# W and its sums stored two pairs at a time: batch 0 of an adapted mixture-of-LoRA kernel

## The chip, the core and the metric

The kernel runs on one core of a Trainium2 chip. The metric is the device time of one execution in microseconds (us), the median of the runs. Five engines are spoken of: PE (TensorE), DVE (VectorE), ACT (ScalarE), POOL (GpSimd) and SP (SyncE), which here only issues DMAs. PE's clock is granted at one of two levels, 1.2 or 2.4 GHz; a granted clock of 1.00 is the higher.

## What is computed

```python
# x (8, 512, 2048), W (2048, 2048), all float32
x = x + einsum('bnr,bor->bno', einsum('bni,bri->bnr', x, B0[ids]), A0[ids])     # rank 16
base = einsum('btd,od->bto', x, W)
logits = einsum('btd,ed->bte', x, Wr) + 5 * one_hot(language_ids)
gates = scatter(softmax(top_2(logits)))                                        # 8 experts
h = einsum('btd,erd->bter', x, A)
out = x + base + 2 * einsum('bter,bte,eor->bto', h, gates, Bm)
```

## The kernel before

Each float32 operand is split into a high and a low part (float32r), and each product is three matmuls: high by high, low by high, high by low (`three_products`). Batches 1 to 7 multiply x and W (plus the identity, for the residual x) by a scheme with seven products over halves instead of eight. The seven combinations of blocks of W that it needs are made in batch 0 and stored in the internal tensor `t_scr`; each later batch reads them back as 56 pairs and 4 LoRA pairs (`pair_load`).

Batch 0 runs over 36 slots, four chunks of nine: in slot i, PE multiplies pair i by the whole of x (`first_products`, 24 matmuls of 512 columns), and slots 8, 17, 26 and 35 are LoRA slots (`first_gated`, 12 matmuls). Everything else is laid out around these slots by hand, in `pe_main`, `act_main`, `dve_main` and `sp_main`, and every engine runs its own list in order:

- SP loads raw W for slot i+5 in slot i (`first_load`, L602, four pieces; L598, two pieces of the LoRA rows from `bt_scr`) into one of two buffers, `raw[:, g % 2]`. It also loads x of batch 1 (`x_load`, L280, eight pieces in each of slots 4 to 7 and 10 to 21) and stores finished output (L763).
- PE transposes W for slot i+3 in slot i in two halves (`w_transpose`, L626): the first half at the head of the slot, the second in the middle.
- ACT copies the transposed blocks to one of two kept places (`w_keep`, L637); DVE makes four sums of the blocks (`w_sums`, L646 to L651) into `tst`; SP stores the direct blocks (`w_store`, L660 and L661) and the sums (`w_sums_store`, L666).
- ACT and DVE split pair i+2 in slot i into high and low parts (`pair_hi`, L715, and `pair_lo`, L719) in a ring of three places. `pair_hi(g)` waits until PE has used pair g-3.
- In slots 9 to 25 the x of batch 1 is turned (`x_turn`), split (`x_hi`, `x_lo`) and multiplied with the small weights (`aux_products`).
- DVE adds the identity to a loaded block of W where it lies on the diagonal (`add_identity`, L612).

The loads wait like this, where `c_wl` counts the low parts made and `c_wt` the halves transposed:

```python
            if g >= 2:
                if (g - 2) % 9 == 8:
                    e.wait_ge(c_wl, g - 1)
                else:
                    e.wait_ge(c_wt, 2 * w_number(g - 2) + 2)
```

`w_number(g)` numbers the pairs without the LoRA ones. `SLOTS0` is 36.

Of the kernel before, what the change touches and what calls it, by code (L numbers as in the profile page):

```python
# [5 lines left out]
def adapted_moe_lora_kernel(nc, x, adapter_ids, language_ids, A0, B0, W, Wr, A, Bm, out):  # L6
# [42 lines left out]
    t_scr = nc.dram_tensor("t_scr", (NI, 2, KP, P, 2, CW), f32, kind="Internal").ap()  # L49
# [16 lines left out]
    LAST = pair_of(NB, 0)  # L66

# [21 lines left out]
    with ctx:  # L89
# [60 lines left out]
        wh = sb("wh", [P, RING, 2, CW], f32r)  # L150
        wl = sb("wl", [P, RING, 2, CW], f32r)
# [14 lines left out]
        gxl, gx = late[:, 0:NAUX], late[:, 256:256 + NAUX]  # L166
        gs = [late[:, 512 + 256 * s:512 + 256 * s + NAUX] for s in range(2)]
# [135 lines left out]

        def x_hi(e, n, u):
# [324 lines left out]
        def w_keep(e, g, h):  # L629
            w = w_number(g)  # L630
            if h == 0 and w >= 2:
                before = g - 2 - (g % 9 < 2)
                e.wait_ge(c_wl, before + 1)
                e.wait_ge(c_t, 4 * w - 4)
                e.wait_ge(d_bs[w % 2], 32 * (w // 2))
            e.wait_ge(c_wt, 2 * w + h + 1)
            e.copy(w_kept(g)[:, h, :], pb[:, 6 + h, :]).then_inc(c_wc, 1)  # L637

        def w_sums(e, g):
            w = w_number(g)  # L640
            b11, b12 = w_kept(g)[:, 0, 0:HT], w_kept(g)[:, 0, HT:CW]
            b21, b22 = w_kept(g)[:, 1, 0:HT], w_kept(g)[:, 1, HT:CW]
            e.wait_ge(c_wc, 2 * w + 2)
            if w:
# [899 lines left out]
```

## Time and profile before

| | |
|---|---|
| median of 3 runs | 1641.58 us (1640.65 to 1642.41) |
| the profiled execution | 1641.15 us |
| its span | 1639.3 us |
| PE busy | 1587.2 us, 97% of the span |
| DVE busy | 1185.9 us, 72% |
| ACT busy | 751.0 us, 46% |
| DMA, mean over the span | 214 GB/s |
| mean granted clock of PE | 0.989 |

The profile is of one execution. Busy shares are means over stages with different limits: batch 0 ends near 355 us, and the seven later batches take about 183 us each. A row of the timeline gives start, duration, engine, line and operation, and in brackets the idle time of the engine just before it and what ended it.

### The profile page before, as it was taken

How to read it: one execution, taken by the hardware profiler on the slowest of the kernel's cores; microseconds unless marked ns; L12 is line 12 of the kernel's file. 1: busy time of each engine (PE TensorE's matmuls, PEld its weight loads, DVE VectorE, ACT ScalarE, POOL GpSimd, SP SyncE). 2: the span in 40 equal slices, each digit the busy share in tenths (PEclk: the TensorE clock that was granted, in tenths of full speed). 3: DMA queues.
4: the chain of work that ended last, by engine and by line, in shares of the span. 5: the costliest groups of instructions: out<-in, count | busy, mean ns of one | idle time of the engine just before them, and what ended most of it. 6: DMA issues, size and time to landing. Idle time of an engine off the chain costs nothing.

```text
span 1639.3 us, 21144 instructions
## 1 busy us (share of the span) xinstructions
PE 1587.2 (97%) x7680; PEld 1333.1 (81%) x7680; DVE 1185.9 (72%) x1615; ACT 751.0 (46%) x984; POOL 10.1 (1%) x19
## 2 busy tenths in 40 slices
PE   7798989999999999999999999999999999999998
PEld 5676768778888888888888888888888888888887
DVE  3674444578769877788769877788769877787665
ACT  4553233335544544445444544445444544445443
POOL 1100000000000000000000000000000000000000
PEclk9898999999999999999999999999999999999999
DMA  8689888968967787878878798878877798566664
GB/s 247 187 218 220 190 194 195 229 211 216 218 199 232 218 232 200 227 227 222 210 205 234 211 233 203 220 236 216 212 207 234 212 241 196 198 226 209 207 220 160
DMA packets 429626, 351.32 MB, mean 214 GB/s; under 512 B 285210, under 2 KB 358218, under 8 KB 428490
## 3 DMA queue, kind: packets, MB, share of 16 engines
q1 hardware_dynamic: 427346, 345.77, 77.7%
q10 hardware_dynamic: 2176, 4.19, 0.9%
q8 instruction: 61, 1.00, 0.3%
q14 instruction: 43, 0.35, 0.1%
HBM read 280.62 MB, written 68.82 MB: 213 GB/s over the span
## 4 chain that ended last, share of the span: by engine, by line
PE 85%; SPq 6%; DMA 4%; DVE 2%; ACT 1%; issue 1%; ACTq 0%; DVEq 0%
PE pb L724 25%; PE pb L723 25%; PE pb L725 25%; PE pb L337 4%; PE pb L339 3%; SPq L602 2%; SPq L280 2%; PE pb L491 2%; DMA raw<-in_L_cond_W_dram 1%; DMA t_scr<-tst 1%; PE pb L626 1%; DMA wrn<-in_L_cond_Wr_dram 1%; DMA t_scr<-raw 0%; SPq L666 0%; DMA bt_scr<-bt 0%
## 5 line engine op out<-in xcount | busy, mean ns | idle before, releaser
L715 ACT CAST wh<-raw 128x1024 fp32r<-128x1024 f32 (+1 forms) x456 | 477.1, 1046 | 684.2 <-PE pb L725 678.4
L719 DVE TENSOR_TENSOR wl<-raw,wh 128x1024 fp32r<-128x1024 f32 (+1 forms) x456 | 554.7, 1216 | 299.2 <-ACT wh L715 298.9
L723 PE MATMUL pb<-wh,sh 128*128 128x512 f32 x1568 | 612.8, 391 | 0.5 <-DVE ost L759 0.5
L724 PE MATMUL pb<-wl,sh 128*128 128x512 f32 x1568 | 611.5, 390 | 0.0
L725 PE MATMUL pb<-wh,sl 128*128 128x512 f32 x1568 | 611.1, 390 | 0.0
L725 PEld LDWEIGHTS pb<-wh,sl 128*128 128x128 f32 x1568 | 294.3, 188 | 62.7
L723 PEld LDWEIGHTS pb<-wh,sh 128*128 128x128 f32 x1568 | 294.5, 188 | 56.2 <-DVE wl L719 0.9
L724 PEld LDWEIGHTS pb<-wl,sh 128*128 128x128 f32 x1568 | 294.6, 188 | 55.0
L337 PE MATMUL pb<-awb,xah 128*128 128x304 f32 x512 | 138.5, 304 | 2.7 <-DVE aux L352 1.6
L339 PE MATMUL pb<-awb,xal 128*128 128x256 f32 x512 | 134.5, 280 | 0.0
L723 PE MATMUL pb<-wh,xh 128*128 128x512 f32 x256 | 109.0, 426 | 1.1 <-DVE xl L513 1.1
L724 PE MATMUL pb<-wl,xh 128*128 128x512 f32 x256 | 104.7, 409 | 0.0
L725 PE MATMUL pb<-wh,xl 128*128 128x512 f32 x256 | 104.2, 407 | 0.0
L337 PEld LDWEIGHTS pb<-awb,xah 128*128 128x128 f32 x512 | 96.3, 188 | 7.6 <-DVE aux L352 1.8
L339 PEld LDWEIGHTS pb<-awb,xal 128*128 128x128 f32 x512 | 96.3, 188 | 4.2
L565 DVE TENSOR_TENSOR sl<-pool_a,sh 128x512 fp32r<-128x512 f32 x120 | 82.1, 685 | 0.0
L637 ACT COPY raw<-pb 128x512 f32<-128x512 f32 x64 | 37.5, 588 | 93.4 <-PE pb L626 50.6
L560 ACT CAST sh<-pool_a 128x512 fp32r<-128x512 f32 x120 | 73.5, 613 | 0.0
L316 DVE TENSOR_TENSOR xal<-pool_a,xah 128x512 fp32r<-128x512 f32 x88 | 60.3, 686 | 15.9 <-ACT xah L311 15.6
L498 DVE TENSOR_TENSOR pool_a<-pool_a,pb 128x512 f32<-128x512 f32 x88 | 59.3, 681 | 11.7 <-PE pb L491 11.7
L626 PE MATMUL pb<-ident,raw 128*128 128x128 f32 x256 | 41.3, 286 | 26.8 <-DMA raw<-in_L_cond_W_dram 17.5
L311 ACT CAST xah<-pool_a 128x512 fp32r<-128x512 f32 x88 | 54.5, 621 | 26.0 <-DVE pool_a L264 16.0
(135 smaller groups left out, 1277.3 us busy)
## 6 DMA issues: line engine op xcount, KB each, us to landing
raw<-t_scr SPq DMA_DIRECT2D x392, 512.0 KB, 4.3
xst<-in_x_dram SPq DMA_DIRECT2D x896, 32.0 KB, 3.6
raw<-in_L_cond_W_dram SPq DMA_DIRECT2D x128, 128.0 KB, 4.2
t_scr<-tst SPq DMA_DIRECT2D x32, 512.0 KB, 5.4
raw<-bt_scr SPq DMA_DIRECT2D x28, 512.0 KB, 3.7
out_dram<-ost SPq DMA_DIRECT2D x28, 512.0 KB, 4.3
out_dram<-u SPq DMA_DIRECT2D x28, 512.0 KB, 3.4
t_scr<-raw SPq DMA_DIRECT2D x32, 256.0 KB, 2.9
```

What stands on the lines that cost most here:

```text
L316: e.tensor_tensor(out=xal[:, u % 2, :, :].rearrange("p k t -> p (k t)"), in0=two(n, q, kp), in1=xah[:, u % 2, :, :].rearrange("p k t -> p ...
L337: e.matmul(pb[:, 4 + t, 0:2 * AW], xah[:, u % 2, k, toks], cols[:, 0:2 * AW], start=u % 8 == 0 and k == 0, stop=False)
L339: last = e.matmul(pb[:, 4 + t, 0:LOW], xal[:, u % 2, k, toks], cols[:, 0:LOW], start=False, stop=u % 8 == 7 and k == 1)
L498: e.tensor_tensor(out=two(n, q, kp), in0=two(n, q, kp), in1=pb[:, delta_bank(n, u), :], op=ALU.add)\
L560: e.copy(sh[:, h % SR, :, :].rearrange("p k t -> p (k t)"), two(b, SUM_QUARTER[product], kp)).then_inc(c_sph, 1)
L565: e.tensor_tensor(out=sl[:, h % SR, :, :].rearrange("p k t -> p (k t)"), in0=two(b, SUM_QUARTER[product], kp), in1=sh[:, h % SR, :, :].rea ...
L626: last = e.transpose(pb[:, 6 + h, j * P:(j + 1) * P], w_raw(g)[:, j, h, :], ident[:, :])
L715: e.copy(pair_split(wh, g), pair_source(g)).then_inc(c_wh, 1)
L719: e.tensor_tensor(out=pair_split(wl, g), in0=pair_source(g), in1=pair_split(wh, g).bitcast(f32), op=ALU.subtract).then_inc(c_wl, 1)
L723: e.matmul(o, h, wh[:, g % RING, k, :], start=start, stop=False)
L724: e.matmul(o, h, wl[:, g % RING, k, :], start=False, stop=False)
L725: return e.matmul(o, l, wh[:, g % RING, k, :], start=False, stop=stop)
```

## The change

Two pairs of W (two slots) share a kept place and a store. A kept place, and the buffers of the sums, hold for each block the columns of both pairs side by side, so that a store writes runs of 2048 bytes where it wrote 1024; `t_scr` is laid out accordingly, and batches 1 to 7 read each half-pair as two runs of 256 words. There is a second kept pair of places (`kept1`), and it lies where one of the three places of the ring was: during batch 0 the ring of split parts has two places, `pair_hi` and `pair_lo` of pair i+1 stand in slot i, and from batch 1 on it has three again. The sums have two buffers of two sums each (`tst`, `tst1`); `tst1` lies over the second buffer of the split x, so batch 1's x is split in one buffer. `gs` and `gx` move into `bt`, and `late` into `ost`. In `sp_main` the load of pair 8 goes behind that of pair 9.

```diff
@@ ring @@
+    def ring(g):
+        return g % 2 if g < SLOTS0 else g % RING
+
+    def ring_before(g):
+        return g - 2 if g < SLOTS0 + 2 else g - RING
@@ places @@
-    t_scr = nc.dram_tensor("t_scr", (NI, 2, KP, P, 2, CW), f32, kind="Internal").ap()
+    t_scr = nc.dram_tensor("t_scr", (NI, 2, KP, P, 2, 2, HT), f32, kind="Internal").ap()
-        wh = sb("wh", [P, RING, 2, CW], f32r)
-        wl = sb("wl", [P, RING, 2, CW], f32r)
+        sb("places", [P, 2, 2, CW], f32, s5)
+        kept1 = sb("kept1", [P, 2, 2, CW], f32, s5)
+        whl = sb("whl", [P, 2 * RING, 2, CW], f32r)
+        def w_high(n):
+            return whl[:, n, :, :]
+        def w_low(n):
+            return whl[:, (4, 5, 3)[n], :, :]
-        gxl, gx = late[:, 0:NAUX], late[:, 256:256 + NAUX]
-        gs = [late[:, 512 + 256 * s:512 + 256 * s + NAUX] for s in range(2)]
+        gxl, gx = bt[:, HO:HO + NAUX], bt[:, HO + 256:HO + 256 + NAUX]
+        gs = [bt[:, HO + 512 + 256 * s:HO + 512 + 256 * s + NAUX] for s in range(2)]
@@ x_hi @@
-            if 16 * n + u >= 2:
+            if n == 1:
+                e.wait_ge(c_ax, 16 + u)
+            elif 16 * n + u >= 2:
                 e.wait_ge(c_ax, 16 * n + u - 1)
@@ w_keep @@
-            if h == 0 and w >= 2:
-                before = g - 2 - (g % 9 < 2)
+            if h == 0 and w >= 4 and w % 2 == 0:
+                before = g - 3 - (g % 9 < 3)
                 e.wait_ge(c_wl, before + 1)
-                e.wait_ge(c_t, 4 * w - 4)
-                e.wait_ge(d_bs[w % 2], 32 * (w // 2))
+                e.wait_ge(c_t, 4 * (w - 2))
+                e.wait_ge(d_bs[w // 2 % 2], 32 * (w // 4))
@@ w_sums @@
-            if w:
-                e.wait_ge(d_ts, 16 * w)
+            if w == 0:
+                e.wait_ge(c_ax, 16)
+            elif w % 2 == 0:
+                e.wait_ge(d_ts, 32 * (w // 2))
@@ w_store, w_sums_store @@
-            e.dma_start(w_place(g, 0, 2), w_kept(g)[:, :, 0:HT]).then_inc(d_bs[w % 2], 16)
-            e.dma_start(w_place(g, 6, 1), w_kept(g)[:, 1:2, HT:CW]).then_inc(d_bs[w % 2], 16)
+            kept = w_kept2(g).rearrange("p h o w n -> p h o (w n)")
+            e.dma_start(w_place(g, 0, 2), kept[:, :, 0, :]).then_inc(d_bs[w // 2 % 2], 16)
+            e.dma_start(w_place(g, 6, 1), kept[:, 1:2, 1, :]).then_inc(d_bs[w // 2 % 2], 16)
-            e.dma_start(w_place(g, 2, 4), tst[:, :, :]).then_inc(d_ts, 16)
+            for n in range(2):
+                e.dma_start(w_place(g, 2 + 2 * n, 2), w_sum2(n)).then_inc(d_ts, 16)
@@ pair_hi @@
-            if g >= RING:
-                wait_used(e, g - RING)
+            if g == SLOTS0 + 2:
+                e.wait_ge(c_wl, SLOTS0 - 1)
+                e.wait_ge(c_t, 4 * 32)
+                e.wait_ge(d_bs[1], 32 * 8)
+            elif g >= 2:
+                wait_used(e, ring_before(g))
@@ three_products @@
+        def part(place_of, g, k):
+            t = place_of(ring(g))
+            if g >= SLOTS0 and not is_lora(*place(g)):
+                return t.rearrange("p a (k n) -> p k a n", k=2)[:, k, :, :]
+            return t[:, k, :]
-            e.matmul(o, h, wh[:, g % RING, k, :], start=start, stop=False)
+            e.matmul(o, h, part(w_high, g, k), start=start, stop=False)
...
@@ bt_copy @@
             e.wait_ge(c_bt, q + 1)
+            if q == 0:
+                e.wait_ge(c_ax, 16)
+                e.wait_ge(d_gs, 32)
+                e.wait_ge(d_ag, 48)
@@ dve_start @@
             pair_lo(e, 0)
-            w_sums(e, 0)
...
             g_lo(e)
+            w_sums(e, 0)
             w_sums(e, 1)
@@ sp_start @@
             first_load(e, 2)
-            w_store(e, 0)
-            w_sums_store(e, 0)
             first_load(e, 3)
             w_store(e, 1)
...
-            w_store(e, 2)
@@ act_main; dve_main has the same with pair_lo @@
-                pair_hi(e, i + 2)
+                if i:
+                    pair_hi(e, i + 1)
@@ sp_main @@
-                if i + 2 < SLOTS0 and (i + 2) % 9 != 8:
+                if i + 2 < SLOTS0 and (i + 2) % 9 != 8 and w_number(i + 2) % 2:
                     w_sums_store(e, i + 2)
...
-                if i + 5 < SLOTS0:
+                if i == 4:
+                    first_load(e, 9)
+                    first_load(e, 8)
+                elif i + 5 < SLOTS0 and i != 3:
                     first_load(e, i + 5)
...
-                if i + 3 < SLOTS0 and (i + 3) % 9 != 8:
+                if i + 3 < SLOTS0 and (i + 3) % 9 != 8 and w_number(i + 3) % 2:
                     w_store(e, i + 3)
```

The instructions move on SP's queue at two places. In slots 3 to 5 the list of before reads as follows; L598 is the load of pair 8, which waits for `bt_scr` (`d_bt`), and the L602 behind it is W(9).

```order
L1042 DMA bt_scr<-bt 128x2048 [waits c_btc]
L1046 DMA bt_scr<-late 128x1024 [waits c_btc]
L598 DMA raw<-bt_scr 128x256 [waits d_bt,c_wt]
L598 DMA raw<-bt_scr 128x256
L660 DMA t_scr<-raw 128x2x256 [waits c_wc]
L661 DMA t_scr<-raw 128x256
L666 DMA t_scr<-tst 128x4x256 [waits c_t]
L602 DMA raw<-in_L_cond_W_dram 128x2x128 [waits c_wt]
L602 DMA raw<-in_L_cond_W_dram 128x2x128 x3
```

The same stretch of SP's list in the changed kernel (L648 is the load of W, L644 that of pair 8, L305 a piece of x, L709, L710 and L716 the stores), as far as W(10), the L648 that waits for `c_wl`:

```order
L1109 DMA bt_scr<-bt 128x2048 [waits c_btc]
L1113 DMA bt_scr<-ost 128x1024 [waits c_btc]
L648 DMA raw<-in_L_cond_W_dram 128x2x128 [waits c_wt]
L648 DMA raw<-in_L_cond_W_dram 128x2x128 x3
L644 DMA raw<-bt_scr 128x256 [waits d_bt,c_wt]
L644 DMA raw<-bt_scr 128x256
L305 DMA xst<-in_x_dram 32x8x32 [waits c_bt]
L305 DMA xst<-in_x_dram 32x8x32 x7
L709 DMA t_scr<-kept 128x2x512 [waits c_wc]
L710 DMA t_scr<-kept 128x512
L716 DMA t_scr<-tst 128x2x512 [waits c_t]
L648 DMA raw<-in_L_cond_W_dram 128x2x128 [waits c_wl]
```

W(9) now stands ahead of pair 8, and the stores are wider and come once in two slots.

DVE's list in slots 6 and 7 of before, where the `wl` of 128x512 is the low part of pair 8 and the `wl` behind it that of pair 9:

```order
L719 TENSOR_TENSOR wl<-raw,wh 128x512 [waits c_wh]
L498 TENSOR_TENSOR pool_a<-pool_a,pb 128x512 [waits c_dl]
L513 TENSOR_TENSOR xl<-pool_a,xh 128x2x256 [waits c_h0]
L438 TENSOR_TENSOR gate<-ohw 128x32 [waits c_gd]
L441 TENSOR_TENSOR auxl<-aux,gate 128x128 [waits c_gd]
L441 TENSOR_TENSOR auxl<-aux,gate 128x128 x3
L719 TENSOR_TENSOR wl<-raw,wh 128x1024 [waits c_wh]
L646 TENSOR_TENSOR tst<-raw 128x256 [waits d_ts,c_wc]
```

DVE's list at the same place in the changed kernel (L775 is `pair_lo`):

```order
L775 TENSOR_TENSOR whl<-kept,whl 128x1024 [waits c_wh]
L530 TENSOR_TENSOR pool_a<-pool_a,pb 128x512 [waits c_dl]
L545 TENSOR_TENSOR xl<-pool_a,xh 128x2x256 [waits c_h0]
L470 TENSOR_TENSOR gate<-ohw 128x32 [waits c_gd]
L473 TENSOR_TENSOR auxl<-aux,gate 128x128 [waits c_gd]
L473 TENSOR_TENSOR auxl<-aux,gate 128x128 x3
L775 TENSOR_TENSOR whl<-raw,whl 128x512 [waits c_wh]
L693 TENSOR_TENSOR tst<-raw 128x256 [waits d_ts,c_wc]
```

The low part of pair 8 (128x512) has moved from slot 6 to slot 7, behind the small operations.

## Rows read from the trace of the kernel before

**Rows 1.** Stretches: us; busy PE, PEld, DVE, ACT, POOL; clock, DMA share, GB/s

```profile
120.00:262.00 142.00, 121.46 (x595) 100.76 (x594) 66.56 (x131) 43.98 (x67) 0.00 (x0) 0.93 0.94 201
...
300.00:345.00 45.00, 41.43 (x204) 34.33 (x203) 29.02 (x74) 12.43 (x19) 0.00 (x0) 0.96 0.85 205
...
500.00:700.00 200.00, 200.00 (x961) 168.60 (x960) 161.06 (x211) 96.55 (x121) 0.00 (x0) 1.00 0.79 219
```

**Rows 2.** PE's waits, 120 to 345 us: total, times, longest

```profile
PE pb L626 <- DMA raw<-in_L_cond_W_dram: 11.3, 5, 4.1
PE pb L626 <- DVE raw L612: 6.5, 1, 6.5
PE pb L491 <- DVE aux L399: 3.1, 1, 3.1
```

**Rows 3.** PE in order of time: transposes of W, and two matmuls

```profile
123.86 1.11 PE L626 MATMUL pb<-ident,raw 128*128 128x128 f32 x4 [3.27 <-DMA raw<-in_L_cond_W_dram]
...
132.14 0.60 PE L626 MATMUL pb<-ident,raw 128*128 128x128 f32 x4
...
138.56 0.60 PE L626 MATMUL pb<-ident,raw 128*128 128x128 f32 x4
...
148.89 1.08 PE L626 MATMUL pb<-ident,raw 128*128 128x128 f32 x4 [6.51 <-DVE raw L612]
...
157.77 0.60 PE L626 MATMUL pb<-ident,raw 128*128 128x128 f32 x4
...
205.30 0.40 PE L725 MATMUL pb<-wh,xl 128*128 128x512 f32 x1
205.53 0.39 PE L723 MATMUL pb<-wh,xh 128*128 128x512 f32 x1
...
206.22 0.60 PE L626 MATMUL pb<-ident,raw 128*128 128x128 f32 x4
...
213.66 0.60 PE L626 MATMUL pb<-ident,raw 128*128 128x128 f32 x4
...
222.61 1.12 PE L626 MATMUL pb<-ident,raw 128*128 128x128 f32 x4 [4.11 <-DMA raw<-in_L_cond_W_dram]
...
231.99 0.63 PE L626 MATMUL pb<-ident,raw 128*128 128x128 f32 x4
```

**Rows 4.** SP's queue in order of time, slots 14 and 19

```profile
200.44 1.92 SPq L602 DMA_DIRECT2D raw<-in_L_cond_W_dram  x4
...
242.38 0.47 SPq L661 DMA_DIRECT2D t_scr<-raw  x1
242.89 0.45 SPq L666 DMA_DIRECT2D t_scr<-tst  x1
243.38 2.98 SPq L602 DMA_DIRECT2D raw<-in_L_cond_W_dram  x4
246.41 4.11 SPq L280 DMA_DIRECT2D xst<-in_x_dram  x8
```

**Rows 5.** Who waited for the stores, whole span: total, times, longest

```profile
DVE tst L646 <- DMA t_scr<-tst: 61.5, 20, 5.6
...
ACT raw L637 <- DMA t_scr<-raw: 34.6, 11, 6.7
```

**Rows 6.** SP's own waits, whole span

```profile
SPq L595 <- DMA bt_scr<-bt: 4.1, 1, 4.1
...
SPq L602 <- DVE wl L719: 3.7, 2, 2.3
```

**Rows 7.** ACT and DVE in order of time, the split of pair 17

```profile
194.77 0.62 ACT L715 CAST wh<-raw 128x512 fp32r<-128x512 f32 x1 [4.58 <-PE pb L725]
...
199.76 0.65 DVE L719 TENSOR_TENSOR wl<-raw,wh 128x512 fp32r<-128x512 f32 x1
```

**Rows 8.** The pieces of W (L602): time to landing

```profile
DMA to landing us min/median/max: 2.2/4.2/6.6
```

**Rows 9.** SP's queue at the start: the rows stored out of `late`

```profile
80.47 2.11 SPq L1225 DMA_DIRECT2D a0g<-late  x3
```

More of the change, by code:

```diff
@@ L302, in x_keep, with x_part @@
             e.copy(two(0, q, kp), pb[:, 6 + u % 2, :]).then_inc(c_xc, 1)
+        def x_part(n, u, part):
+            return xa(0 if n == 1 else u)[:, part, :, :]
         def x_hi(e, n, u):
@@ L310, in x_hi @@
                 e.wait_ge(d_bt, 16)
-            e.copy(xah[:, u % 2, :, :].rearrange("p k t -> p (k t)"), two(n, q, kp)).then_inc(c_xh, 1)
+            if n == 2 and u == 1:
+                e.wait_ge(d_ts, 32 * 16)
+            e.copy(x_part(n, u, 0).rearrange("p k t -> p (k t)"), two(n, q, kp)).then_inc(c_xh, 1)
         def x_lo(e, n, u):
@@ L315, in x_lo @@
             e.wait_ge(c_xh, 16 * n + u + 1)
-            e.tensor_tensor(out=xal[:, u % 2, :, :].rearrange("p k t -> p (k t)"), in0=two(n, q, kp),
-                            in1=xah[:, u % 2, :, :].rearrange("p k t -> p (k t)").bitcast(f32), op=ALU.subtract)\
+            e.tensor_tensor(out=x_part(n, u, 1).rearrange("p k t -> p (k t)"), in0=two(n, q, kp),
+                            in1=x_part(n, u, 0).rearrange("p k t -> p (k t)").bitcast(f32), op=ALU.subtract)\
              .then_inc(c_xl, 1)
@@ L639, in w_sums @@
         def w_sums(e, g):
             w = w_number(g)
[L641 to L642 removed]
+            b11, b12, b21, b22 = (w_kept(g)[:, h, o, :] for h in range(2) for o in range(2))
             e.wait_ge(c_wc, 2 * w + 2)
[L644 to L647 removed]
+            if w == 0:
+                e.wait_ge(c_ax, 16)
+            elif w % 2 == 0:
+                e.wait_ge(d_ts, 32 * (w // 2))
@@ L712, in pair_hi @@
                 e.wait_ge(c_wc, 2 * w_number(g) + 2)
-            if g >= RING:
-                wait_used(e, g - RING)
-            e.copy(pair_split(wh, g), pair_source(g)).then_inc(c_wh, 1)
+            if g == SLOTS0 + 2:
[4 more added lines that the diff above has]
+                wait_used(e, ring_before(g))
+            e.copy(pair_split(w_high, g), pair_source(g)).then_inc(c_wh, 1)
         def pair_lo(e, g):
             e.wait_ge(c_wh, g + 1)
-            e.tensor_tensor(out=pair_split(wl, g), in0=pair_source(g), in1=pair_split(wh, g).bitcast(f32),
+            e.tensor_tensor(out=pair_split(w_low, g), in0=pair_source(g), in1=pair_split(w_high, g).bitcast(f32),
                             op=ALU.subtract).then_inc(c_wl, 1)
+        def part(place_of, g, k):
+            t = place_of(ring(g))
+            if g >= SLOTS0 and not is_lora(*place(g)):
+                return t.rearrange("p a (k n) -> p k a n", k=2)[:, k, :, :]
+            return t[:, k, :]
         def three_products(e, o, h, l, g, k, start, stop):
-            e.matmul(o, h, wh[:, g % RING, k, :], start=start, stop=False)
-            e.matmul(o, h, wl[:, g % RING, k, :], start=False, stop=False)
-            return e.matmul(o, l, wh[:, g % RING, k, :], start=False, stop=stop)
+            e.matmul(o, h, part(w_high, g, k), start=start, stop=False)
+            e.matmul(o, h, part(w_low, g, k), start=False, stop=False)
+            return e.matmul(o, l, part(w_high, g, k), start=False, stop=stop)
         def first_products(e, i, h):
@@ L1325, in act_main @@
                 for i in range(SLOTS):
+                    if b == 1 and i == 0:
+                        pair_hi(e, SLOTS0 + 1)
                     if pair_of(b, i) + 2 < LAST:
@@ L1353, in dve_main @@
                     x_turn(e, 1, i - 9)
-                pair_lo(e, i + 2)
+                if i:
+                    pair_lo(e, i + 1)
                 if i == 4:
@@ L1403, in dve_main @@
                         x_turn(e, n, X_AT[i])
+                    if b == 1 and i == 0:
+                        pair_lo(e, SLOTS0 + 1)
                     if pair_of(b, i) + 2 < LAST:
```

61 lines of the change are left out of this document (39 added, 22 removed).

## The prediction

> **What bounds it now.** I read the page first, where the tensor engine (PE) is busy nearly throughout, and then cut the span into stretches. From batch 1 on PE never rests: 200 us busy in 200, clock 1.00. Between 120 and 262 us, which is slots 6 to 21 of batch 0, it is busy 121.5 of 142 us at a granted clock of 0.93, and in 300:345 it is busy 41.4 of 45 at 0.96 [rows 1]. Idle time is 20.5 and 3.6 us; the clock costs another 0.07 x 142 = 9.9 and 0.04 x 45 = 1.8. So batch 0 holds all that can be won here: 30.4 + 5.4 = 35.8 us, of which I leave 0.5 alone. 35.3 us is the most that this change can give.
>
> The list of PE's waits names the cause: 11.3 us for loads of W and 6.5 us for the identity that VectorE (DVE) adds to a loaded block [rows 2]. The order in time of the transposes (L626, first half of slot i+3 at the head of slot i) gives slot lengths. A slot of `first_products` alone takes 138.56 - 132.14 = 6.4 us, one with `aux_products` 213.66 - 206.22 = 7.4 us, and slot 8, a LoRA slot, 148.89 - 6.51 - 138.56 = 3.8 us. After a wait the slot is long as well: 231.99 - 222.61 = 9.4 behind a 4.1 us wait, 157.77 - 148.89 = 8.9 (against 6.4) behind 6.5 us [rows 3]. So an idle stretch of 4 to 6.5 us costs 2.0 to 2.5 us more at the lower clock.
>
> Why are loads of W late? The SP queue's rows show it issuing without a pause: three stores at 0.45 to 0.47, four pieces of W 2.98, eight pieces of x 4.11, with gaps 8.6 us for a slot [rows 4], against PE's 7.4. From slot 15 on it has fallen behind by more than a slot.
>
> **What the change removes.** Two stores of direct blocks and two of sums now serve two slots, four issues instead of six, with half the runs of memory. Per slot SP has 2.0 (W, as at 200.44, where no large store stands ahead), 4.1 (x) and half of four stores at about 0.5, so 1.0: 7.1 us, at most 7.5 if W stays near 2.5. That is PE's pace. Slots 10 to 15 then stay level, and the losses of slots 15 to 22 are owed to the queue no more. DVE's 61.5 us and ScalarE's (ACT) 34.6 us of waiting for stores [rows 5] mostly go too: odd sums wait for no store, and a kept place comes free after four pairs. Two of these waits reach PE: the identity of slot 9, and the 3.1 us of slot 29, where `aux_final(1)` stands behind the stalled sums. At slot 4, W(9) no longer queues behind the load of pair 8, which held SP for 4.1 us [rows 6]; W(9) then goes out some 4 us earlier, and slot 6 loses its 3.3 us wait [rows 3]. If nothing new came, all 35.3 us would go.
>
> The Trainium skill (DMA: Bandwidth & Descriptors, "Issuing engines are not separate DMA queues") says of the time to initiate a DMA that it "is usually small relative to the DMA itself". By that rule fewer issues would give nothing, none of the relief of slots 15 to 22 would come, and the sum would be that of the third rival below, 1652. This trace disagrees: 8.6 us of issue in a 7.4 us slot.
>
> **What it adds: the LoRA slots.** This is the largest term. With two places for the split parts instead of three, `pair_lo(i+1)` stands in slot i, where `pair_lo(i+2)` stood. `first_load(g)` with g = 10, 19, 28 waits for the low part of pair g-2 (8, 17, 26), which is read from the buffer that the load overwrites. Before, that split followed the end of slot g-5; now it follows the end of slot g-4, since it needs the place of pair g-4. But W(g) is transposed at the head of slot g-3. PE therefore reaches the transpose with the load not even issued, at the heads of slots 7, 16 and 25. The trace of before has the same chain one slot earlier: ACT's cast at 194.77, DVE's difference 199.76 + 0.65, SP's issue at 200.44 for 1.92 us, and the transpose at 206.22 without a wait [rows 7, 4, 3]; SP waited there before too, 3.7 us in two waits [rows 6]. Now the chain starts where PE stops: 0.1 + 0.62 (cast) + 0.05 + 0.65 (difference) + 0.05 + 1.4 (three issues) + landing of the fourth. Landing of a piece of W is 2.2 us at least and 4.2 in the median [rows 8]; SP has been blocked for most of two slots, so little stands in the queues, and I take 2.8. That is 5.7 us, between 5.1 and 7.1, and 2.3 for the clock: 8.0 each, **24.0 us for three** (22.2 to 28.8).
>
> Everything behind the blocked load on SP is late too. Count from PE's stop at slot 7: load 10 ends at 3.4, x at 7.4, load 11 at 9.4, adapter rows (three issues, 1.3) and x at 14.7, load 12 at 16.7, landed at 20.9, its identity 0.5: 21.4. PE wants it at 5.7 + (6.4 + 2.3) + 3.8 = 18.2. It waits 3.2 and loses 1.5 in clock: **4.7 us** (0 to 8). Behind slot 16 the same count gives load 22 out at 24.0, since the sums of pair 19 (DVE at 20.9) and x stand ahead; landed 28.2; DVE adds its identity only after the even sums, which wait for a store issued by 22.0 (landed near 26.9, an estimate from [rows 8]), so at 29.7, against a wish for 27.6: 2.1 + 1.4 = **3.5 us** (0 to 7). Behind slot 25 no x octets follow and nothing is late.
>
> **The small terms.** At the start `bt_copy(0)` now waits for the rows that SP stores out of the same tensor. SP issued the first of them at 80.47 for 2.11 us [rows 9]; DVE's second set of sums now comes before that, about 1.7 us more, and PE's second set of transposes waits for the copy. On the other side ACT's third kept block no longer waits for a store. I take 1.0 us lost (0 to 3). The shorter ring costs PE nothing elsewhere: a full pair is twice the width of the LoRA pair's 0.62 and 0.65 [rows 7], so its parts are there about 2.6 us after the slot begins at most, under the 3.8 of the shortest. The single buffer for the parts of x (batch 1) lets ACT start after the aux products of the same slot, about 5 us in, and the next aux products are 6 us later: hidden, though a full slot of cover is gone. The even sums may hold DVE until a store lands, but nothing that PE wants within 5 us is behind them. In batches 1 to 7 the moving operand is two runs of 256 words instead of one of 512. No row shows such a matmul; its bounds are nothing and one more instruction boundary: 0.23 us from one start to the next (205.30 to 205.53 in [rows 3]) less 512 columns at 2.4 GHz, 0.213, so 17 ns. I take nothing, as the engine reads the same words at the same step.
>
> **The sum.** 35.3 - 24.0 - 4.7 - 3.5 - 1.0 = 2.1 us won. The profiled execution took 1641.15 us around a span of 1639.3, the median of the runs is 1641.58, 0.4 above it. I forecast 1639.5 us: no change that a measurement can tell, since about 0.2% (3.3 us) is what it resolves.
>
> **Rivals.**
> - *The late loads cost nothing beyond the three waits.* For it: DMA traffic has drained while SP was blocked, so pieces land nearer 2.2 than 4.2 us, and each wait is 5.1 + 2.3. Against it: x and W then go out back to back. 35.3 - 22.2 - 1.0 = 12.1 won: 1629.5. Chance 0.22.
> - *Slower: the waits at slots 7, 16 and 25.* If load g lands like the slow ones (6.6 us, the largest in [rows 8]), each wait is 9.5 + 2.5 = 12, three are 36, and with the other terms the balance is 35.3 - 36 - 9.2 = -9.9: 1651.5. It decides from (35.3 + 3.3 - 9.2)/3 = 9.8 us each. Against it is the drained queue. Chance 0.15.
> - *The relief does not come.* The queues move what they moved, with a DMA share of 0.94 [rows 1]; if bytes and not issues set SP's 8.6 us, the losses of slots 15 to 22 (30.4 less 9.0 for slot 9 and about 5.2 for slot 6, so 16.2) stay, less the 3.5 counted above: 12.7 us worse than my sum, 1652. Against it: the same four pieces of W took 1.92 us in one place and 2.98 behind the wide store in another [rows 4], so what stands ahead on the queue counts. It is also what the page's rule on issue time would make of it. Chance 0.12.
> - *The split moving operand costs.* 17 ns x 4704 matmuls = 80 us, 1719; at 1 ns it is 5 us. Against it: nothing in the trace has shown a price for strides. Chance 0.05.
>
> My forecast has 0.46, spread over 1633 to 1646. **Faster** by over 0.2% (below 1638.3) takes the first rival and 0.20 of the forecast: 0.42. **Same**: 0.20 of the forecast, 0.04 of the third rival and 0.02 of the second: 0.26. **Slower**: 0.06 of the forecast, 0.13 of the second rival, 0.08 of the third and the operand's 0.05: 0.32. The range leaves out the operand and the tails: 1629 to 1652; the forecast alone has 1633 to 1646.
>
> **What the profile will show.** Right: PE waits of 5 to 7 us for W at three places about 80 us apart, the transposes of pairs 10, 19 and 28; no wait at slots 6 and 29; SP rows with pauses between slots 10 and 13; batches 1 to 7 as busy as before, with 0.23 us from matmul to matmul. Wrong: waits at the LoRA slots under 4 us or over 9; SP without pause in slots 17 to 21; DVE's even sums ahead of a late `pair_lo` that PE waits for; a longer matmul L725.

## The result and the profile after

The changed kernel takes 1650.26 us, the median of 5 runs (1647.14 to 1652.38), against 1641.44 us for the kernel before beside it (1640.65 to 1642.41). The ratio is 1.0052, with an interval from 1.0038 to 1.0067: **slower by 8.6 us, 0.5%**. The forecast was 1639.5 us. The execution that was profiled took 1652.38 us, the slowest of the five, against 1641.15 us for the profile of before, so the two traces differ by 11.2 us and not by 8.6.

The stretches of the changed kernel's trace (columns as in [rows 1]) show where:

```profile
120.00:262.00 142.00, 118.64 (x576) 98.45 (x575) 64.90 (x129) 41.95 (x65) 0.00 (x0) 0.92 0.71 193
300.00:345.00 45.00, 41.75 (x219) 34.88 (x218) 25.40 (x65) 16.75 (x28) 0.00 (x0) 1.00 0.84 242
262.00:300.00 38.00, 32.47 (x156) 27.22 (x156) 13.27 (x23) 9.56 (x16) 0.00 (x0) 0.91 0.49 154
500.00:700.00 200.00, 200.00 (x962) 168.56 (x961) 160.04 (x218) 96.33 (x121) 0.00 (x0) 1.00 0.83 221
```

Idle time and clock together, (stretch - busy) + (1 - clock) x stretch, were 30.4 us between 120 and 262 us [rows 1]; now they are 23.4 + 11.4 = 34.8. The stretch 262:300, which had nothing to lose (busy 37.59 of 38 us before), now loses 5.5 + 3.4 = 8.9. That is some 13 us more, less 2 us won in 300:345, which is the 11 us between the two traces. Batches 1 to 7 are as before. The DMA engines meanwhile have become less busy, 0.71 where they had 0.94 [rows 1].

PE's waits from 120 to 345 us answer to [rows 2]:

```profile
PE pb L672 <- DMA raw<-in_L_cond_W_dram: 25.5, 7, 5.5
PE pb L672 <- issue: 3.3, 3, 2.1
PE pb L786 <- DVE ost L824: 1.9, 1, 1.9
```

The two waits for DVE of before, 6.5 and 3.1 us, are gone by name (what that is worth is told below). Two small ones are new: 1.9 us for DVE's copy of finished output in slot 18, and 1.0 us for a low part of x (L545). They stand in lora_buffer too, and no run tells which part of the change brings them. Three waits of the transposes, 3.3 us in all, are listed as "issue", which means that the profile names nobody. The wait for W has grown from 11.3 to 25.5 us. In order of time (the transposes of W, L672, the place of L626 in [rows 3]):

```profile
121.11 0.60 PE L672 MATMUL pb<-ident,raw 128*128 128x128 f32 x4
...
134.30 1.11 PE L672 MATMUL pb<-ident,raw 128*128 128x128 f32 x4 [4.89 <-DMA raw<-in_L_cond_W_dram]
...
148.27 0.63 PE L672 MATMUL pb<-ident,raw 128*128 128x128 f32 x4 [2.35 <-DMA raw<-in_L_cond_W_dram]
...
158.55 1.12 PE L672 MATMUL pb<-ident,raw 128*128 128x128 f32 x4 [3.42 <-DMA raw<-in_L_cond_W_dram]
...
210.58 1.12 PE L672 MATMUL pb<-ident,raw 128*128 128x128 f32 x4 [5.37 <-DMA raw<-in_L_cond_W_dram]
...
254.52 1.12 PE L672 MATMUL pb<-ident,raw 128*128 128x128 f32 x4 [3.23 <-DMA raw<-in_L_cond_W_dram]
...
291.67 1.12 PE L672 MATMUL pb<-ident,raw 128*128 128x128 f32 x4 [5.53 <-DMA raw<-in_L_cond_W_dram]
```

134.30, 210.58 and 291.67 are the heads of slots 7, 16 and 25, 76 and 81 us apart. Their chain, at slot 7, on ACT, DVE and SP (the place that [rows 7] show one slot earlier):

```profile
129.07 0.62 ACT L771 CAST whl<-raw 128x512 fp32r<-128x512 f32 x1 [3.45 <-PE pb L788]
...
129.72 0.69 DVE L775 TENSOR_TENSOR whl<-raw,whl 128x512 fp32r<-128x512 f32 x1 [2.82 <-ACT whl L771]
...
130.44 1.91 SPq L648 DMA_DIRECT2D raw<-in_L_cond_W_dram  x4
```

The cast waits for PE's last matmul on the old occupant of the place, the difference follows, then SP issues, and the transpose starts 3.9 us after SP began. SP's own waits for that low part, from 60 to 345 us, answer to [rows 6]: 23.5 us where 3.7 us stood.

```profile
SPq L648 <- DVE whl L775: 23.5, 3, 9.2
```

### The profile page after: what moved, and what is told of

It reads as the page before. It is cut to its first block, busy times and chain, and to the rows that moved or that the text cites. A ratio compares the mean times of both kernels' runs of the same rounds, so it can differ in the third digit from the quotient of the medians.

```text
span 1650.5 us, 21070 instructions
## 1 busy us (share of the span) xinstructions
PE 1591.0 (96%) x7680; PEld 1336.1 (81%) x7680; DVE 1187.2 (72%) x1615; ACT 750.9 (45%) x984; POOL 9.7 (1%) x19
## 4 chain that ended last, share of the span: by engine, by line
PE 89%; SPq 3%; DMA 2%; DVE 2%; ACT 2%; issue 1%; ACTq 0%; DVEq 0%
PE pb L786 26%; PE pb L787 26%; PE pb L788 26%; PE pb L369 4%; PE pb L371 3%; PE pb L523 2%; SPq L648 2%; DMA raw<-in_L_cond_W_dram 2%; PE pb L672 1%; SPq L305 1%; DMA wrn<-in_L_cond_Wr_dram 1%; DVE whl L775 0%; ACT xa L343 0%; DMA t_scr<-tst 0%; DVE pool_a L530 0%
## 5 line engine op out<-in xcount | busy, mean ns | idle before, releaser
L771 ACT CAST whl<-raw 128x1024 fp32r<-128x1024 f32 (+1 forms) x440 | 460.3, 1046 | 645.3 <-PE pb L788 645.2
L775 DVE TENSOR_TENSOR whl<-raw,whl 128x1024 fp32r<-128x1024 f32 (+1 forms) x440 | 535.0, 1216 | 286.3 <-ACT whl L771 286.1
L786 PE MATMUL pb<-whl,sh 128*128 128x512 f32 x1568 | 612.9, 391 | 0.5 <-DVE ost L824 0.5
L787 PE MATMUL pb<-whl,sh 128*128 128x512 f32 x1568 | 611.6, 390 | 0.0
L788 PE MATMUL pb<-whl,sl 128*128 128x512 f32 x1568 | 611.2, 390 | 0.0
L788 PEld LDWEIGHTS pb<-whl,sl 128*128 128x128 f32 x1568 | 294.3, 188 | 62.9
L786 PEld LDWEIGHTS pb<-whl,sh 128*128 128x128 f32 x1568 | 294.5, 188 | 56.2 <-DVE whl L775 0.9
L787 PEld LDWEIGHTS pb<-whl,sh 128*128 128x128 f32 x1568 | 294.6, 188 | 55.0
L369 PE MATMUL pb<-awb,xa 128*128 128x304 f32 x512 | 138.5, 304 | 2.9 <-DVE aux L384 1.6
L371 PE MATMUL pb<-awb,xa 128*128 128x256 f32 x512 | 134.4, 280 | 0.0
L786 PE MATMUL pb<-whl,xh 128*128 128x512 f32 x256 | 110.1, 430 | 3.3 <-DVE ost L824 1.9
L787 PE MATMUL pb<-whl,xh 128*128 128x512 f32 x256 | 105.1, 410 | 0.0
L369 PEld LDWEIGHTS pb<-awb,xa 128*128 128x128 f32 x512 | 96.4, 188 | 7.9 <-DVE aux L384 1.8
L371 PEld LDWEIGHTS pb<-awb,xa 128*128 128x128 f32 x512 | 96.3, 188 | 4.3
L672 PE MATMUL pb<-ident,raw 128*128 128x128 f32 x256 | 42.5, 293 | 34.2 <-DMA raw<-in_L_cond_W_dram 30.9
L672 PEld LDWEIGHTS pb<-ident,raw 128*128 128x128 f32 x256 | 32.3, 150 | 40.3 <-DMA raw<-in_L_cond_W_dram 35.5
```

The lines of the kernel that those rows point to most:

```text
L369: e.matmul(pb[:, 4 + t, 0:2 * AW], x_part(n, u, 0)[:, k, toks], cols[:, 0:2 * AW], start=u % 8 == 0 and k == 0, stop=False)
L371: last = e.matmul(pb[:, 4 + t, 0:LOW], x_part(n, u, 1)[:, k, toks], cols[:, 0:LOW], start=False, stop=u % 8 == 7 and k == 1)
L672: last = e.transpose(pb[:, 6 + h, j * P:(j + 1) * P], w_raw(g)[:, j, h, :], ident[:, :])
L771: e.copy(pair_split(w_high, g), pair_source(g)).then_inc(c_wh, 1)
L775: e.tensor_tensor(out=pair_split(w_low, g), in0=pair_source(g), in1=pair_split(w_high, g).bitcast(f32), op=ALU.subtract).then_inc(c_wl, 1)
L786: e.matmul(o, h, part(w_high, g, k), start=start, stop=False)
```

## The experiments

All medians are of 3 rounds or more; ratios are to the kernel before, run beside each. One microsecond is 0.06%.

**lora_buffer.** The chain above is taken apart: the LoRA rows go where nothing else is at that time, so that the loads of pairs 10, 19 and 28 wait for transposes alone.

```diff
             if g >= 2:
-                if (g - 2) % 9 == 8:
-                    e.wait_ge(c_wl, g - 1)
-                else:
-                    e.wait_ge(c_wt, 2 * w_number(g - 2) + 2)
+                e.wait_ge(c_wt, 2 * w_number(g - 2 if (g - 2) % 9 != 8 else g - 4) + 2)
...
-                if k == 8:
+                if k == 8 and g < 35:
+                    e.dma_start(lora_raw(g)[:, w * HT:(w + 1) * HT], bt_scr[:, w, c * HT:(c + 1) * HT])\
+                     .then_inc(d_lr, 16)
...
+        def lora_raw(g):
+            if g == 8:
+                return xa0[:, 0, :, :].rearrange("p k t -> p (k t)").bitcast(f32)
+            return bxt[:, :].bitcast(f32)
```

> The changed kernel with one edit: the LoRA rows of pairs 8, 17 and 26 go to memory of their own (free at that time), so that the loads of pairs 10, 19 and 28 no longer wait for pair_lo(8), (17), (26). Theory A (the new waits at slots 7, 16, 25 and the queue held behind them ate the gain): the three waits (15.8 us idle, about 22 with the clock) and most of the follow-up waits at slots 9, 10 and 18 to 19 (some 12 to 17 us) go: 1650 less 30 to 35, so 1615 to 1622 us. Rival B (SP is the bound anyway: the pauses at the three slots only take the place of lateness that the queue would have run up in slots 15 to 22, where the kernel before lost 16 us): the three waits go, but waits for W of some 10 to 15 us come up in slots 15 to 22: 1634 to 1640 us.

Measured: 1631.85 us (1630.46 to 1632.62), ratio 0.9934 (0.992 to 0.9947). By the ratios that is 1.18% or 19 us below the changed kernel (18.4 by the medians), and it is 10.7 us below the kernel before. PE's waits from 120 to 345 us:

```profile
PE pb L683 <- DMA raw<-in_L_cond_W_dram: 11.9, 6, 2.9
PE pb L683 <- issue: 3.0, 3, 2.4
```

The wait for W falls by 13.6 us. At the heads of slots 7, 16 and 25 stand 1.7, 2.2 and 0 us where 4.9, 5.4 and 5.5 stood. The time lies between the two expectations: the three waits went almost wholly, but waits of 1.6 to 2.9 us stay at slots 9, 10 and 21 (2.93 and 2.79 the largest), so the queue's own lateness is there as rival B said.

**before_lora_buffer.** The same edit in the kernel before (with `xah` for `xa0`).

> The kernel before with the same edit (memory of their own for the LoRA rows of pairs 8, 17, 26). Theory A: nothing waited there on PE and SP stood only 3.7 us at these loads, so 1638 to 1642 us, within 0.2% of before. Rival C (the two buffers for W were short before as well, and a freer queue is worth something whatever the change): 1625 to 1635 us, and then most of what the buffer gives to the changed kernel would not be due to the shorter ring.

Measured: 1642.04 us, ratio 1.0000 (0.9991 to 1.0009), as theory A had it. The buffer is worth nothing there. So its 19 us undo something that the change brought.

**ring_two_alone.** The kernel before with one part of the change, the ring of two places in batch 0.

```diff
+    def ring(g):
+        return g % 2 if g < SLOTS0 else g % RING
...
-            if g >= RING:
-                wait_used(e, g - RING)
+            if g >= 2:
+                wait_used(e, ring_before(g))
...
-                pair_hi(e, i + 2)
+                if i:
+                    pair_hi(e, i + 1)
```

> The kernel before with the ring of two places in batch 0 and nothing else of the change: pair_hi and pair_lo of pair i+1 in slot i, stores and kept places as they were. Theory A (the ring of two alone makes the waits of the loads of pairs 10, 19 and 28 on the split of the LoRA pair, and these cost 15 to 20 us net of lateness that the queue has anyway, since buffer_unpaired, which lacks only this wait, stood at 1641 and unpaired at 1658): 1655 to 1662 us, with waits of 5 us or more of PE at the heads of slots 7, 16 and 25. Rival (the waits come from another part of the change and were only removed with the buffer; or a queue that is late anyway absorbs them): 1640 to 1648 us. Unlike the changed kernel this one also has its kept places freed one slot later (w_keep of pair i+3 waits for pair_lo(i+1)), which can add waits of its own within slots.

Measured: 1661.64 us, ratio 1.0114 (1.0099 to 1.013), slower by 18.7 us. The transposes in order of time have the same waits, here those of slots 7 and 25:

```profile
137.24 1.12 PE L632 MATMUL pb<-ident,raw 128*128 128x128 f32 x4 [4.81 <-DMA raw<-in_L_cond_W_dram]
...
300.66 1.11 PE L632 MATMUL pb<-ident,raw 128*128 128x128 f32 x4 [5.22 <-DMA raw<-in_L_cond_W_dram]
```

Slot 16 has 5.35 us. From 120 to 345 us PE waits 28.3 us for W where before had 11.3, and 15.4 of these 28.3 stand at the three slots. One part alone costs what the buffer gives back. That is the cause of the slower time: without this wait (lora_buffer) the changed kernel is faster than the kernel before.

**load_behind.** SP gets something to do instead of waiting.

```diff
-                elif i + 5 < SLOTS0 and i != 3:
+                elif i + 5 < SLOTS0 and i != 3 and i not in (5, 14, 23, 6, 15, 24):
                     first_load(e, i + 5)
...
                     x_load(e, 1, (i - 6) // 2, (i % 2 * 2, i % 2 * 2 + 1))
+                if i in (6, 15, 24):
+                    first_load(e, i + 5)
+                    first_load(e, i + 4)
```

> The changed kernel with SP's order alone changed: the loads of pairs 10, 19 and 28 stand one slot later, behind the x pieces and the load of pair 11, 20, 29, so that SP has nothing held up behind its wait for pair_lo(8), (17), (26). Theory A: the waits at slots 7, 16, 25 stay at 5 to 6 us each, since nothing before them changed, and the follow-up waits at slots 9, 10, 18 and 19 go: 1650 less 10 to 15, so 1635 to 1640 us. Rival B (the queue's throughput is the bound in slots 9 to 20, not what is held up): the follow-up waits stay or move by a slot: 1647 to 1652 us.

Measured: 1655.15 us, ratio 1.0078 (1.0064 to 1.0092), slower than the changed kernel. Theory A's expectation fails here. The follow-up waits did go (at slots 9 and 10 stand 0.7 us each for 2.4 and 3.4), but the waits at slots 7 and 16 did not stay at 5 us. They became 11.5 and 10.2 us. SP's rows at slots 5 and 6 say why:

```profile
125.44 5.18 SPq L305 DMA_DIRECT2D xst<-in_x_dram  x8
130.79 1.25 SPq L951 DMA_DIRECT2D a0g<-a_scr  x3
132.08 3.87 SPq L305 DMA_DIRECT2D xst<-in_x_dram  x8
136.00 13.29 SPq L648 DMA_DIRECT2D raw<-in_L_cond_W_dram  x12
```

The low part that W(10) waits for was ready at 131.7 us, but SP was still issuing what now stood ahead, and W(11) after it; the last row holds the loads of three pairs, and W(10)'s went out at 138.04. The wait at slot 25, where no x stands ahead, stayed at 5.2 us. The pause did not go either: behind W(10) SP stood 7.3 us until PE had transposed pair 10, inside the last row, and in all it waited 34.8 us for transposes (14.1 in the changed kernel) and 2.3 instead of 23.5 for low parts. So this order moved the pause and made it longer; it does not show that no order could fill it.

**unpaired.** The changed kernel without its purpose: stores for one pair at a time, in runs of 1024 bytes, in every slot.

```diff
-            e.dma_start(w_place(g, 0, 2), kept[:, :, 0, :]).then_inc(d_bs[w // 2 % 2], 16)
+            e.dma_start(w_place(g, 0, 2)[:, :, cols], w_kept(g)[:, :, 0, :]).then_inc(d_bs[w // 2 % 2], 16)
...
-                e.dma_start(w_place(g, 2 + 2 * n, 2), w_sum2(n)).then_inc(d_ts, 16)
+                e.dma_start(w_place(g, 2 + 2 * n, 2)[:, :, cols], w_sum2(n)[:, :, cols]).then_inc(d_ts, 16)
```

> The changed kernel with its stores made in every slot again, for one pair at a time in runs of 1024 bytes (two stores of direct blocks and two of sums in each slot, four issues where the change has four for two slots); ring, kept places, buffers and the layout in t_scr stay those of the change. So it differs from the changed kernel by the pairing alone. If issues or runs set SP's time (my prediction): SP takes some 1.0 us more a slot in slots 10 to 22, PE waits for W there and the time is 10 us or more above the changed kernel: 1660 us and above. If bytes set SP's time (the third rival of the prediction): 1648 to 1654 us, as the changed kernel.

Measured: 1658.12 us, ratio 1.0096 (1.008 to 1.0111), 7 to 8 us above the changed kernel. So pairing is worth something, though less than the reading by issues and runs had it (1660 us and above). A slot of the unpaired kernel in SP's queue (near slot 12), direct stores, sums, W, x:

```profile
174.62 0.45 SPq L709 DMA_DIRECT2D t_scr<-raw  x1
175.12 0.47 SPq L710 DMA_DIRECT2D t_scr<-raw  x1
175.64 0.98 SPq L717 DMA_DIRECT2D t_scr<-tst  x2
176.66 2.25 SPq L648 DMA_DIRECT2D raw<-in_L_cond_W_dram  x4
178.96 4.14 SPq L305 DMA_DIRECT2D xst<-in_x_dram  x8
```

And two slots of the paired one (lora_buffer, where SP doesn't pause):

```profile
190.63 0.45 SPq L720 DMA_DIRECT2D t_scr<-kept  x1
191.12 0.47 SPq L721 DMA_DIRECT2D t_scr<-kept  x1
191.64 1.64 SPq L727 DMA_DIRECT2D t_scr<-tst  x2
193.31 3.65 SPq L659 DMA_DIRECT2D raw<-in_L_cond_W_dram  x4
197.01 3.92 SPq L306 DMA_DIRECT2D xst<-in_x_dram  x8
200.97 1.99 SPq L659 DMA_DIRECT2D raw<-in_L_cond_W_dram  x4
203.01 4.69 SPq L306 DMA_DIRECT2D xst<-in_x_dram  x8
```

A quartet of W costs 1.99 us behind x and 3.65 us behind a pair's sums. Two unpaired slots spend 2 x (0.92 + 0.98 + 2.25 - 1.99) = 4.3 us on stores, two paired ones 0.92 + 1.64 + 3.65 - 1.99 = 4.2. By these rows alone SP's pace looks the same. Over more slots it isn't. From the load of W(11) to that of W(20), nine slots in which the kernels issue the same loads and store the same bytes, lora_buffer takes SP 69.2 us (131.78 to 200.97, above) and its unpaired twin, the next experiment, 72.2, with 0.3 us of waiting in each. First lora_buffer's start, then both ends of the twin:

```profile
131.78 1.99 SPq L659 DMA_DIRECT2D raw<-in_L_cond_W_dram  x4
```

```profile
133.28 1.99 SPq L659 DMA_DIRECT2D raw<-in_L_cond_W_dram  x4
...
205.48 1.99 SPq L659 DMA_DIRECT2D raw<-in_L_cond_W_dram  x4
```

That is 0.33 us a slot. The unpaired and the changed kernel have the same difference where the LoRA waits don't disturb it: 50.5 against 48.3 us for six slots from W(11), 0.35 us a slot. So pairing does work by way of SP, at a third of the 1.0 us a slot that was expected. The DMA engines differ as well: share 0.84 unpaired and 0.71 paired from 120 to 262 us, and the median landing of a piece of W. First unpaired, then the changed kernel, which answers to [rows 8]:

```profile
DMA to landing us min/median/max: 2.1/3.6/6.6
```

```profile
DMA to landing us min/median/max: 2.2/2.7/6.6
```

**buffer_unpaired.** Both edits.

> Both edits at once: LoRA rows in memory of their own, and stores of one pair in every slot in runs of 1024 bytes. What is left of the change is the ring of two places, the second pair of kept places, the buffers of sums, the moved load of pair 9 and the strided operand. If pairing is worth the same with and without the LoRA wait (8 us, from 1650 and 1658) and the buffer the same with and without pairing (18 us): 1658 - 18 = 1640 us, the time before, and then the rest of the change is worth nothing either way. If the LoRA waits only hid lateness of the unpaired queue (it waits for W 45 us in all, before 17.5): 1648 to 1655 us. If part of the pairing's worth comes only when the queue is not held up: over 1642 us as well, with the pairing worth more than 10 us.

Measured: 1641.16 us, ratio 0.9991 (0.9982 to 1.0), as the first expectation had it (1640). (The execution profiled took 1644.48 us, the slowest of eleven.) So the four kernels form a square. The LoRA wait costs 1.18% paired and 1.05% unpaired (19 and 17 us), the pairing gives 0.57% with the buffer and 0.44% without (9 and 7 us), and what is left of the change (order of SP, kept places, buffers of sums, operand) is -0.09%: 1.5 us won, with an interval from 0 to 3 us.

**split_stores.** The changed kernel with every store of two blocks as two stores.

```diff
-                e.dma_start(w_place(g, 2 + 2 * n, 2), w_sum2(n)).then_inc(d_ts, 16)
+                for s in range(2):
+                    e.dma_start(w_place(g, 2 + 2 * n + s, 1), w_sum2(n)[:, s:s + 1, :]).then_inc(d_ts, 16)
```

> The changed kernel with each store of two blocks made as two stores of one block, runs of 2048 bytes as they are: seven issues for a pair of pairs where the change has four (unpaired: eight for two slots), same bytes, same runs. It asks what the pairing's 8 us are made of. If the number of issues (my prediction's reading): three more issues of 0.47 us in two slots, half to all of the way to the unpaired kernel, 1654 to 1658 us. If the length of the runs, by which the DMA engines are busy and a piece of W lands late (median landing of W 2.5 us paired, 4.0 unpaired; DMA share 0.71 and 0.84 between 120 and 262 us): 1649 to 1652 us, and W lands as in the changed kernel, in 2.5 us.

Measured: 1650.02 us, ratio 1.0039 (1.0025 to 1.0052), the changed kernel's time with three issues more. The issues alone are worth nothing; four stores of sums take SP 2.46 us and the W behind 1.92 to 2.3, so the cost only moves from one row to the next: the six slots from W(11) take SP 48.2 us, and 48.3 in the changed kernel. W lands in 2.6 us in the median and the DMA share is 0.70, both as in the changed kernel. So the 7 to 9 us of pairing are not made by fewer issues. They come with longer runs, with stores in every second slot, with 0.33 us less of SP's time a slot and with earlier landings; longer runs and rarer stores were not tried apart.

**half_sums.** Half of the bytes of the sums (two of four blocks are not stored, and the later batches read the other two in their place).

```diff
-                e.dma_start(w_place(g, 2 + 2 * n, 2), w_sum2(n)).then_inc(d_ts, 16)
+                e.dma_start(w_place(g, 2 + 2 * n, 1), w_sum2(n)[:, 0:1, :]).then_inc(d_ts, 16)
```

> The changed kernel with half of the bytes of the sums: of the four blocks two are stored (and batches 1 to 7 read these two in place of the other two, so that the result of those batches is not the reference's), same number of issues. If bytes set what a store costs SP: the two issues take 0.9 us instead of 1.57 and the four pieces of W behind them 2.0 to 2.5 instead of 3.65, some 2 us less in two slots. If the issue is a fixed cost: 1.5 us and 3.6 us as they are. On the time: the LoRA waits do not depend on it, so 1640 to 1646 us if a freer queue shortens the waits at slots 9, 10, 18 and 20, and 1649 to 1652 us if these come from the held-up queue alone.

Measured: 1638.53 us, ratio 0.9970 (0.9958 to 0.9982), some 12 us below the changed kernel by the medians, 13 by the ratios, and below both ranges that were expected, with the LoRA waits where they were (4.8, 5.4 and 5.3 us). The store of sums and the W behind it, in SP's queue:

```profile
221.98 1.52 SPq L716 DMA_DIRECT2D t_scr<-tst  x2
223.55 2.49 SPq L648 DMA_DIRECT2D raw<-in_L_cond_W_dram  x4
```

The two issues themselves did not get cheaper, yet two stores of the same size take 0.98 us in the unpaired kernel: an issue's own row doesn't go by its bytes, and what sets it stays open. The W behind them did get cheaper, by 1.2 us, which speaks for bytes. Neither expectation holds alone. The six slots from W(11) take SP 44.4 us instead of 48.3, 0.65 us less a slot, so the bytes of the stores weigh more in the queue than how they are cut. The waits at slots 10 and 21 fell from 3.4 and 3.2 to 1.9 and 0.6 us.

**buffer_w_first.** On lora_buffer, the load of W goes ahead of the store of sums.

```diff
-                if i + 2 < SLOTS0 and (i + 2) % 9 != 8 and w_number(i + 2) % 2:
-                    w_sums_store(e, i + 2)
                 if i == 3:
...
                     first_load(e, i + 5)
+                if i + 2 < SLOTS0 and (i + 2) % 9 != 8 and w_number(i + 2) % 2:
+                    w_sums_store(e, i + 2)
```

> The kernel with the LoRA rows in memory of their own (1631.9 us) and, in SP's order, the load of W ahead of the store of sums in every slot. If what stands ahead on the queue sets what a piece of W costs and when it lands: W takes 2.0 us of SP in every slot instead of 3.65 in every second one, and the waits for W at slots 7 to 10, 15 and 20 (some 11 us) shorten by half: 1623 to 1628 us. If the bytes only move to whatever stands behind the store (x then takes 5.5 us instead of 3.9): 1630 to 1634 us; above that if the later store of sums holds up DVE's next sums and, behind them, the low parts that PE needs.

Measured: 1630.70 us, ratio 0.9922 (0.9909 to 0.9936); 1631.85 lies within the runs (1628.92 to 1632.33). PE's wait for W falls from 16.9 to 9.0 us over batch 0, but its waits under "issue" at the same transposes rise from 3.0 to 5.9 and it now waits 2.9 us for x, so 2 us are left of the 8. The second expectation came: x now stands behind the store.

```profile
192.21 2.66 SPq L659 DMA_DIRECT2D raw<-in_L_cond_W_dram  x4
194.91 0.98 SPq L727 DMA_DIRECT2D t_scr<-tst  x2
195.94 5.29 SPq L306 DMA_DIRECT2D xst<-in_x_dram  x8
```

2.66 + 0.98 + 5.29 = 8.9 us against 1.64 + 3.65 + 3.92 = 9.2 in the other order. The larger part of a store's cost is paid by whoever stands behind it.

**buffer_w_mid.** The same in slots 5 to 25 only.

```diff
+                w_first = 5 <= i < 26
+                if stores and not w_first:
+                    w_sums_store(e, i + 2)
...
+                if stores and w_first:
+                    w_sums_store(e, i + 2)
```

> The kernel with LoRA rows in memory of their own, with the load of W ahead of the store of sums in slots 5 to 25 only; in slots 0 to 4 and from 26 on the order is that of the change. With W first everywhere PE's waits for W fell from 16.9 to 9.0 us, but the start came 1.5 us later, and a wait of 4.5 us stood at slot 29 where 2.4 us stood before. If these two are the price of a later store of sums, this kernel keeps the gain without it: 1626 to 1629 us. If the freed W only meets later x (waits of aux_products for x, 2.9 us in all with W first): 1629 to 1632 us.

Measured: 1630.01 us (1628.20 to 1631.88), ratio 0.9925 (0.9911 to 0.9939). It is the lowest median here, some 12 us below the kernel before, but not told apart from lora_buffer or buffer_w_first. The second expectation holds, and PE's wait for x is there (2.1 us).

## Why the prediction was wrong

**The term for the LoRA waits** was right in place and mechanism. The waits are 4.89, 5.37 and 5.53 us where 5.7 were forecast; the slots behind them are 1.4, 2.5 and 2.8 us longer than 6.4 and 7.4 us, where 2.3 each was forecast. That sums to 22.5 us against 24.0. Taken away, they give back 17 to 19 us, since the queue has some lateness in any case.

**The relief is the step that failed.** "Per slot SP has 2.0 (W ...), 4.1 (x) and half of four stores at about 0.5, so 1.0: 7.1 us, at most 7.5." SP has 8.2 us or more in such a slot. The sums' two issues take 1.6 us instead of 1.0, and the W behind them takes 3.65 us instead of 2.0 to 2.5; x takes 3.9. Before, it was 8.3 to 8.7 (rows at 213.62, 221.89 and 230.33 give 8.3 and 8.4; the 8.6 of [rows 4] is one of the dearer slots). So 1.1 to 1.5 us less a slot was forecast, and over the nine slots from W(11) to W(20) it is about half a microsecond: 74.1 us before, of which SP waited 5.0, and 69.2 in lora_buffer. PE's slots are 7.4 us at most, so SP goes on falling behind. I had read [rows 4] (1.92 us here, 2.98 behind the wide store) as a price of the place in the queue that pairing would halve. It goes mostly with what the store ahead moves: twice the store once in two slots costs nearly as much.

What PE lost shows the same. At the heads of slots 13 to 22 it stood idle 10.8 us before and 5.6 in lora_buffer; half came back, not all. So "if nothing new came, all 35.3 us would go" was too much by more than two thirds: with the LoRA waits out (lora_buffer) the gain is 10.7 us, where the sum without its three waits and follow-ups has 35.3 - 1.0 = 34.3.

**Slot 9 was misread,** and 9.0 us of the relief hung on it. The prediction had the 6.5 us wait for the identity come from DVE's stall behind the store of sums. DVE did stall. But the four pieces of W(12), to which the identity is added, went out from 141.13 us on and took 4.4 to 5.1 us each to land, the last until 148.27, and the identity was added right then:

```profile
146.70 0.42 DVE L646 TENSOR_TENSOR tst<-raw 128x256 f32<-128x256 f32 x1 [5.58 <-DMA t_scr<-tst]
...
148.29 0.49 DVE L612 TENSOR_TENSOR raw<-raw,ident 128x128 f32<-128x128 f32 x2
```

As the load stood, PE would have waited just as long without the stall. The wait was the queue's lateness under another name, and it stayed: in the changed kernel DVE has no stall there and waits for W(12) itself, and PE waits 2.4 and 3.4 us at slots 9 and 10 (2.9 and 1.6 in lora_buffer, 4.7 at slot 9 in buffer_unpaired).

```profile
147.67 0.49 DVE L658 TENSOR_TENSOR raw<-raw,ident 128x128 f32<-128x128 f32 x2 [1.53 <-DMA raw<-in_L_cond_W_dram]
```

**The third rival** ("if bytes and not issues set SP's 8.6 us") named the mechanism of the relief that failed, at 0.12, and at 1652 its time was the nearest. Some of that is luck: it left all of slots 15 to 22 lost, where half came back, and it counted slot 9 as won. It was right for the larger part: halved bytes take 0.65 us a slot off SP's round, three more issues nothing. But not all is bytes, since the same bytes in runs twice as long, stored half as often, take 0.33 us off.

The rule that stood beside that rival (the Trainium skill, DMA: Bandwidth & Descriptors, "Issuing engines are not separate DMA queues") has the time to initiate a DMA "usually small relative to the DMA itself". On the number of issues this case agrees with it: three more in two slots, 1650.02 against 1650.26 us. On the size of one it agrees as well: SP has mostly 0.45 to 0.5 us for an issue, and a piece of W lands after 2.2 to 6.6 us. The prediction held 8.6 us in a slot of 7.4 against it. That is the sum of fifteen issues on one queue, three stores, four pieces of W and eight of x, and the quoted sentence does not speak of such a sum.

**The follow-ups** were named wrongly. Forecast were 4.7 + 3.5 = 8.2 us at slots 9 and 19. Waits of 2.4, 3.4 and 3.2 us stand at slots 9, 10 and 21; but lora_buffer, with no queue held up, has 2.9, 1.6 and 2.8 us there. With half of the sums' bytes they are 2.3, 1.9 and 0.6, though the pauses at the LoRA slots are as they were. They are mostly the queue's own lateness, the relief that did not come.

**Right, as shown:** no wait at slot 6. The unpaired kernel has 0.1 us there, and ring_two_alone, with the order of before, has 2.8, so it was the order of W(9) and pair 8, as the prediction had it. The 3.1 us of slot 29 are gone (2.1 us stand at the head of slot 30 instead). DVE's waits for the stores of sums fell from 61.5 us [rows 5] to 22.8, ACT's 34.6 to nothing. The start costs 0.7 us by the transpose of slot 4 (107.93 against 107.19), for 1.0 forecast. The strided operand costs nothing: in batches 1 to 7 L786 takes 391 ns with it and L723 took 391 without.

**The chances.** The slower case that came was a mixture of my forecast's LoRA term and the third rival. I had priced the relief by one pair of rows, 1.92 and 2.98, of which more than one reading was possible, and gave the reading on which 16 us hung too much belief.

## What to carry to other kernels

A buffer given up in one place to make another wider can move work past the point where a third party needs it; follow each wait that names the moved step, and look whether a few hundred words elsewhere are free at that moment, as here. When a queue is the pacing engine, most of a pause in it is lost for good (17 to 19 us of kernel time for pauses of 23.5), and the reorderings tried here only moved the loss. What an issue costs in a full queue belongs largely to what stands ahead of it, so price a merged store by the queue's whole round over many slots, not by its own rows or by one pair of slots. And before a wait is put down to the engine that is named, look when the data that this engine needed had landed.

## What the runs showed of the hardware

Four 128 KB loads of W occupied SP for 1.99 us behind x, 2.25 behind 512 KB of sums in two stores (unpaired), about 2.75 behind 512 KB in one (2.98 in [rows 4]), and 3.65 behind 1024 KB in two (lora_buffer); eight pieces of x 3.92, and 5.29 behind the sums (buffer_w_first). A store's own issue mostly took 0.45 to 0.82 us. Runs of 2048 for 1024 bytes, in half as many stores, brought DMA's share from 0.92 to 0.78 (buffer_unpaired, lora_buffer) while it moved more a second, 214 against 202 GB/s, and a piece of W landed in 2.8 us for 3.8 in the median. A float32r moving operand in two runs of 256 words streams as fast as one of 512 (391 ns a matmul both ways).
